# One-hot rows, gather products and adds as wide as a group can span, in a two-layer graph kernel

## The reference, cut to what matters

```python
# N = 12500 nodes, 256 channels, E = 200000 edges sorted by dst
dst = minimum((12500 * uniform ** 2.0).astype(int32), 99999); sort(dst)

def _hconv(x, src, dst, ew, w1, b1, w2, b2, g, b):
    h = relu(x @ w1 + b1)
    msg = ew[:, None] * h[src]
    agg = segment_sum(msg, dst, num_segments=x.shape[0])
    h = agg @ w2 + b2
    return relu(_bn(h, g, b))

x = x + gnn(layernorm(x))     # two _hconv layers, each with a batch norm behind it
x = x + ffn(layernorm(x))     # 8 experts of three 256 x 256 products, mixed by a softmax
```

## Time and profile before

| what | value |
|---|---|
| time, median of 3 runs | 4941.79 us (4939.51 to 4956.82) |
| span of the profiled execution | 4946.6 us |
| first layer's input and indices, until the first gather | 0 to 167 us |
| gathers of layer 0 | 167 to 1614 us |
| layer 0's end, batch norms, second w1 | 1614 to 1751 us |
| gathers of layer 1 | 1751 to 3122 us |
| the rest, mostly the feed-forward part | 3122 to 4946 us |
| TensorE, VectorE, ScalarE, GpSimd busy | 91%, 56%, 47%, 46% |

### The profile page before, as it was taken

One profiled execution on the slowest core, in us unless ns is written; L12 is line 12 of the kernel. 1 busy time (PEld: TensorE's weight loads), 2 busy tenths in 40 slices (PEclk: granted clock), 3 DMA queues, 4 the chain that ended last, 5 costly groups with the idle time before them and its releaser, 6 DMA issues. The chain is left out here.

```text
span 4946.6 us, 71609 instructions
## 1 busy us (share of the span) xinstructions
PE 4498.3 (91%) x25653; PEld 3759.5 (76%) x25653; DVE 2774.9 (56%) x6601; ACT 2325.3 (47%) x3935; POOL 2252.2 (46%) x2405
## 2 busy tenths in 40 slices
PE   7779999997999689888989988399999999999999
PEld 6678877786666577667766677388888888888888
DVE  7767777776344763333333333566666666666665
ACT  5755567665011650000000000477777777777777
POOL 1577777777777367777777777500000000000000
PEclk9889999998999899999999999699999999999999
DMA  5579997787665288666766676311101111111010
GB/s 163 173 212 322 322 285 242 247 279 231 222 210 166 85 273 264 214 222 220 244 227 218 217 240 201 115 31 35 25 27 35 35 25 28 35 35 25 27 30 15
DMA packets 642778, 769.61 MB, mean 156 GB/s; under 512 B 270584, under 2 KB 533475, under 8 KB 636022
## 3 DMA queue, kind: packets, MB, share of 16 engines
q1 hardware_dynamic: 328176, 374.22, 22.6%
q0 software_dynamic: 107088, 290.75, 18.9%
q10 hardware_dynamic: 207157, 100.03, 7.3%
HBM read 614.57 MB, written 137.63 MB: 152 GB/s over the span
## 5 line engine op out<-in xcount | busy, mean ns | idle before, releaser
L982 POOL DMA_INDIRECT wst<-h,src_col x1104 | 1070.3, 969 | 346.8 <-issue 326.4
L1034 PE MATMUL pf<-work 128*128 128x288 f32 (+3 forms) x3528 | 1163.6, 467 | 34.9 <-DMA work<-front 34.8
L1034 PEld LDWEIGHTS pf<-work 128*128 128x128 f32 x3528 | 637.3, 193 | 304.1 <-issue 203.0
L1994 DVE TENSOR_TENSOR f_hl<-f_hf,f_hh 128x1024 fp32r<-128x1024 f32 (+1 forms) x400 | 479.9, 1200 | 635.3 <-ACT f_hf L1857 635.0
L1179 ACT ACTIVATE ah<-agg 128x1024 fp32r<-128x1024 f32 (+1 forms) x50 | 51.8, 1037 | 1518.3 <-DVE agg L1318 1517.7
L1850 ACT ACTIVATE f_hh<-f_p,f_sh,f_sc 128x512 fp32r<-128x512 f32 (+1 forms) x800 | 571.1, 767 | 396.4 <-PE f_p L2092 394.6
L1066 PEld LDWEIGHTS ps<-oh,wst 128*128 128x128 f32 x4416 | 570.2, 201 | 180.9 <-DMA wst<-h,src_col 96.5
L1066 PE MATMUL ps<-oh,wst 128*128 128x128 f32 x4416 | 597.5, 288 | 111.2 <-DMA wst<-h,src_col 110.3
L1211 DVE TENSOR_SCALAR oh<-lane,rel_col,ew_col 128x128 f32<-128x128 f32 x2198 | 617.1, 362 | 0.0
L982 POOL DMA_INDIRECT f_xr<-h,src_col x550 | 533.9, 971 | 172.4 <-issue 163.6
L982 POOL DMA_INDIRECT f_u<-h,src_col x544 | 527.4, 969 | 169.5 <-issue 159.4
(11 more groups left out here) (277 smaller groups left out, 7394.4 us busy)
## 6 DMA issues: line engine op xcount, KB each, us to landing
work<-h SPq DMA_DIRECT2D x216, 512.0 KB
work<-front SPq DMA_DIRECT2D x100, 576.0 KB
work<-front SPq DMA_DIRECT2D x50, 1024.0 KB
front<-agg ACTq DMA_DIRECT2D x37, 1200.0 KB
work<-front SPq DMA_DIRECT2D x50, 816.0 KB
front<-agg ACTq DMA_DIRECT2D x25, 1600.0 KB
wst<-h,src_col POOLq DMA_INDIRECT x1104, 3.9
a_x<-in_x SPq DMA_DIRECT2D x24, 512.0 KB, 4.7
```

Source lines behind the costliest of these rows:

```text
L982: g.indirect_dma_start(G[t % R], None, h_dram[layer], bass.IndirectOffsetOnAxis(ap=src_col[:, col:col + 1], axis=0)).then_inc(ga[t % R], 16)
L1034: ins = g.matmul(pF[:, k, 0:count * w].rearrange("p (s c) -> p s c", c=w), HB[a % 2][0:r, n, k * P:(k + 1) * P], x, start=b == 0, stop=b = ...
L1994: g.tensor_tensor(hlo[l][q % 2][:, :, 0:nn], hf[l][:, :, 0:nn], hhi[l][q % 2][:, :, 0:nn].bitcast(fp32), ALU.subtract).then_inc(f_lo[l], 1)
```

## The change

A width is worked out for each group from its position alone: `width(f)` = (f + 14) // 5 + 1, made even. With FGL[layer] + q for f it is 26 to 82 columns in layer 0 and 28 to 82 in layer 1, on average 54 and 55. The one-hot matrix, the moving side and output of the gather product, and the window that VectorE adds have that width instead of 128. The number of instructions stays, but for three in the guard: an iota on POOL (`limit`), and two on VectorE, which mark any group whose span would not fit its width, so that the slow path is taken then. The planner's `other` now counts 16 passes of max(70, 111 x width / 128), which is 16 x 70 or 16 x 71 for every group, in place of 16 x 111.

```diff
+    SLOPE, FLOOR = 5, 15
+
+    def width(f):
+
+        least = (f + FLOOR - 1) // SLOPE + 1
+        return min(least + least % 2, P)
...
+                        g.iota(limit[:, :], pattern=[[P, GB]], base=FLOOR, channel_multiplier=1,
+                               allow_small_or_imprecise_dtypes=True)
...
+                                g.wait_ge(init, 11)
+                                g.scalar_tensor_tensor(limit[:, :], group_max[:, :], float(SLOPE), limit[:, :], ALU.mult,
+                                                       ALU.is_ge).then_inc(idx, 1)
+                                g.wait_ge(idx, WIDE)
                                 g.scalar_tensor_tensor(group_max[0:FG, 0:1], past_c[0:FG, :], float(P), group_max[0:FG, 0:1],
                                                        ALU.mult, ALU.max).then_inc(idx, 1)
                                 g.wait_ge(idx, FAR_MAX)
+                                g.scalar_tensor_tensor(group_max[:, :], limit[:, :], float(P), group_max[:, :],
+                                                       ALU.mult, ALU.max).then_inc(idx, 1)
+                                g.wait_ge(idx, WIDE_MAX)
...
-            other = [16 * 111 + sum(max(224, NB * hot(layer, t)[4] * 9 // 10) for t in hot_behind(layer, q))
+            other = [16 * max(70, 111 * width(FGL[layer] + q) // P) + sum(max(224, NB * hot(layer, t)[4] * 9 // 10) for t in hot_behind(layer, q))
...
+                            wide = width(FGL[layer] + q)
                             for k in range(KC):
                                 for t in tiles_of[q]:
...
-                                    ins = g.matmul(pS[bank_of[q]][:, k, :], G[t % R][:, k * P:(k + 1) * P], OH[t % RO][:, :],
+                                    ins = g.matmul(pS[bank_of[q]][:, k, 0:wide], G[t % R][:, k * P:(k + 1) * P], OH[t % RO][:, 0:wide],
...
-                                ins = g.tensor_scalar(OH[t % RO][:, :], lane[:, :], rel_col[:, col:col + 1], ew_col[:, col:col + 1],
+                                ins = g.tensor_scalar(OH[t % RO][:, 0:wide], lane[:, 0:wide], rel_col[:, col:col + 1], ew_col[:, col:col + 1],
...
-                            win = agg[:, :, bass.ds(base, P)]
+                            wide = width(FGL[layer] + q)
+                            win = agg[:, :, bass.ds(base, wide)]
...
-                            g.tensor_tensor(win, win, pS[bank_of[q]][:, :, 0:P], ALU.add).then_inc(g_add, 1)
+                            g.tensor_tensor(win, win, pS[bank_of[q]][:, :, 0:wide], ALU.add).then_inc(g_add, 1)
```

More of the change, by code:

```diff
@@ L220, in first_layer @@
                 span = sb(s, "span", [P, 1])
+                limit = sb(s, "limit", [P, GB])
                 base_i = sb(s, "base_i", [GB, P], i32)
@@ L251, in first_layer @@
                 GMIN = REL + 2
-                (SEG, SEGC, SHIFT, COL, WINDOW, WINDOW_I, TILE_REL, PAST, KEY_IN, PAST_C, KEY, FAR_MAX,
-                 SPAN) = range(GMIN + 1, GMIN + 14)
+                (SEG, SEGC, SHIFT, COL, WINDOW, WINDOW_I, TILE_REL, PAST, KEY_IN, PAST_C, KEY, WIDE, FAR_MAX, WIDE_MAX,
+                 SPAN) = range(GMIN + 1, GMIN + 16)
                 SPAN_ALL, FAR = SPAN + 1, SPAN + 3
```

## The result

| | before | after |
|---|---|---|
| median | 4941.73 us (4939.51 to 4956.82, 4 runs) | 4994.73 us (4981.84 to 5003.06, 4 runs) |
| ratio of the runs | | 1.0097, 95% interval 1.0079 to 1.0114 |
| span of the profiled execution | 4946.6 us | 4980.0 us |
| TensorE's granted clock over the span | 0.961 | 0.926 |

The account below looks back on a forecast made before the run. The prediction took GpSimd's issue of gathers to bound layer 1 and most of layer 0. Its terms, -2 -4 -1 +0.4 +1 -1, made about -7 us, hence 4935 us against a median of 4941.8; range 4908 to 4970.

Parts of the forecast that it names:

- What bounds: In layer 1 and most of layer 0, GpSimd's issue of gathers sets the end, at 1.251 us a gather.
- the 19 us of waits: GpSimd's waits for gather products beyond its usual gap: all that a faster TensorE could give through free buffers.
- Gather products: On TensorE the weight load sets 0.110 us, so a pass goes from 0.111 to 0.110; -2 us in the sum.
- The term "-1": Narrower gather passes on TensorE at the low clock save 0 to -3 us, taken as -1.
- The clock, "0 to +6, taken +1": In stretches without units TensorE's clock falls, but a group needs 4 to 5 of 5.0 us: 0 to +6, taken +1.
- The clock rival: Clock falls in groups with units; TensorE becomes the bound at 15% low-clock groups; 5050 us at 20%; chance 0.11.
- The planner, "+-3, taken 0": Sheets' units move up to three groups earlier, the work between stays the same: +-3 us, taken 0.
- gathers and sheets collide: Units placed earlier wait longer for sheet loads; three more waits cost 10 us: 4952, counted within the forecast's 0.80.
- Buffers free sooner, -4: Shorter one-hot rows and adds on VectorE free buffers sooner, worth 0 to -8 us, taken as -4.
- gathers beside VectorE, -1: VectorE's work costs a gather at most 2 ns, 4 us in all; a part may go: -1 us.
- Guard: Two 4-column VectorE operations in a chain on which TensorE waits: +0.4 us; chance of tripping into the slow path 0.01.
- The signs named ahead: What the profile after would show: pass times, PE and PEld busy time, row lengths, gather pace, layer stretches, layer 1's clock.

Follow-up runs that it names:

- e7_wide_first: The changed kernel with the planner's old price and 128-column one-hot rows and gather products in layer 0's first 35 groups: 4957.84 us, ratio 1.0029 to the kernel before.
- e13_layer1_old: The changed kernel with the planner's old price, narrow in layer 1 alone, 128 columns in layer 0: 4952.7 us, ratio 1.0000 to the kernel before.
- e5_wide_plan_old: The changed kernel with 128-column gather products and the planner's old price, one-hot rows and adds still narrow: 4941.93 us, ratio 0.9995 to the kernel before.
- e8_at_least_96: The changed kernel with the planner's old price and no width under 96 columns: 4943.0 us, ratio 0.9994 to the kernel before.

## Why the prediction was wrong, point by point

**What bounds.** Right: 1.251 us is the median from one gather to the next in every kernel. The counts beside it were wrong: layer 0 has 1115 gathers and layer 1 has 1083, not 1103 and 1095. At 1.251 us they make 1395 of 1447 us and 1355 of 1371, so the close fit of 1370 to 1371 was an accident. The 68 us over the pace are the 19 us of waits and some 50 us of gathers whose own row is longer than the median, which a faster TensorE doesn't shorten. The 19 us were rightly named as all that is to be had from it. What the sum lacked was the other direction, how much a slower TensorE can take: 39.2 us of waits became 92.5.

**Gather products.** Right at the full clock: 0.107 to 0.111 at 28 to 128 columns. Wrong at the low clock. I scaled the duration of two overlapping loads, 0.50/0.30, to a pitch of 0.18, and so let a narrow pass save 0.04 us. It takes 0.204, the same as a wide one. The term "-1" is 0.

**The clock, "0 to +6, taken +1".** This is the first step that failed. I put the low-clock group without units at 2.9 us of passes and two hot products of 0.5 to 1 us, "4 to 5 of 5.0". Measured: 3.27 + 1.13 + 0.98 = 5.38 us, over the 5.0 that it may take. 35 groups at 0.38 us are 13 us; the gathers behind them come 9 to 12 us late, and e7_wide_first gave back 6 to 10. With what is lost elsewhere in layer 0, which no run places, the term is about 20 us (ratio 1.0042). Both numbers were within reach: the trace of before has sixteen passes at 3.27 us in the same stretch.

**The clock rival** had the right cause and the wrong place. It named the groups with units and a break-even of 15% of layer 1's groups at the low clock. Layer 1's clock of 0.91 is (1 - 0.91)/0.5 = 18%, and e13_layer1_old shows that it costs nothing there. Its price was too high: TensorE's busy share in layer 1 rose from 1218.24/1371 = 0.889 to 1251.48/1367 = 0.915, which is 0.13 us a group for ten points more of low clock, or 1.3 us for a whole group, where I had 3.75. (This is the mean over the groups on which the low clock fell; the price of a group full of units wasn't measured. The rival's +110 us also counts 550 groups for a break-even worked out for layer 1 alone, which has 271.) What I held against it, that a TensorE that lags has no idle time left to lower the clock, is refuted by 143 us without a gap at 0.50. The groups without units, which I had set aside as having room, are those that lost.

**The planner, "+-3, taken 0".** The second step that failed, and nearly as dear: 16 us. The rival "gathers and sheets collide" came near it (a unit placed earlier, three waits, 10 us), but it looked at units that wait for their sheet. What is late is a store, with a sheet's load close to it, and the wait goes through ScalarE's clearing and VectorE's hot add to TensorE. The row was there to be read, in the waits of before in 343 to 1000 us:

```profile
ACT agg L1110 <- DMA front<-agg: 136.0, 30, 10.4
```

**Buffers free sooner, -4, and gathers beside VectorE, -1.** One-hot rows fell to 335 ns on average instead of the 320 forecast, adds to 262 (270 forecast). e5_wide_plan_old has both at 0.9995: 0, or at most 7 us by its interval. **Guard:** did not trip; of its +0.4 nothing can be told (first gather at 167.2 us instead of 166.9, and at 166.6 to 169.2 in all traces).

**The range.** Each of the two losses alone lies inside 4908 to 4970 (4967.69 and 4964.24 us). The range took in either, but no case in which both happen.

**The signs named ahead:** sixteen passes in 1.9 us at any width came true at the full clock (3.45 us at the low one), and so did layer 1's clock of 0.90 or more; 1367 us for layer 1 is one under its 1368 to 1373. PEld "as busy as before" and a slightly lower PE did not come true: they rose by 122 and 114 us. Nor did layer 0's stretch of 1435 to 1450 us (1484).

## What to carry to other kernels

Making the moving side shorter under a weight load that stays as long saved no time in this kernel, at either clock, and TensorE was granted the full clock less of the time; look where TensorE has the least work beside such products, and add up a group there at the low clock, from rows at the low clock. 96 of 128 columns were still enough here; 26 to 34, in the groups that lost, were not. And where loads and stores fill the DMA engines, a plan that moves loads by a few microseconds is a change of its own: count how many stores have a load close to them, see who waits for each store, and time it apart from the rest.

No version tried beats the kernel before: the best that computes the result are e5_wide_plan_old and e8_at_least_96, both at its time.

## What the runs showed of the hardware that I had not expected

- An fp32 gather pass takes 0.204 us at the low clock at 32 and at 128 columns, 0.107 to 0.111 at the full clock from 28 to 128. What these passes have in common is the weight load of 128 columns, at either level.
- With the same number of passes in each group, TensorE was granted 0.80 with 128 columns, 0.79 with 96 and 0.50 with 26 to 34 in 165 to 343 us, though with 26 to 34 it was busy without a gap from 200 us on.
- A store of 1.2 MB took 11.2 us to land with one load of 1.3 MB 3.4 us ahead of it, and 17.1 us with one 2.5 us ahead and another 2.4 us behind. Over 432 stores in twelve traces the mean is 13.5 us with a load in the 2 us before, and 9.8 with none from 2 us before to 3 us behind.
- Ratios of 1.0033 and 0.9966 came from no change to a product, a row or an add, only from when units stand and how much the sheets' loads move.
